# Last layer of a transformer-like chain: int8 rounding without clip and without GpSimd, bias and outlier sums moved, token maxima turned one outlier tile earlier

## The reference, cut to what matters

```python
def _ste_quant_rows(a):
    scale = jnp.maximum(jnp.max(jnp.abs(a), axis=-1, keepdims=True) / 127.0, 1e-08)
    return jnp.clip(jnp.round(a / scale), -127.0, 127.0) * scale

def _linear8bit(x, W, b):
    col_max = jnp.max(jnp.abs(x), axis=tuple(range(x.ndim - 1)))
    outlier = col_max > 3.0
    x_in = jnp.where(outlier, 0.0, x)
    x_out = jnp.where(outlier, x, 0.0)
    return _ste_quant_rows(x_in) @ _ste_quant_rows(W).T + x_out @ W.T + b

h = _linear8bit(x, W1, b1)          # 512 -> 2048
x = x + _linear8bit(h, W2, b2)      # 2048 -> 512
```

## Time and profile before

| | us |
|---|---|
| median of 3 runs | 2096.34 |
| lowest, highest | 2092.91, 2097.01 |
| the profiled execution | 2093.76 |
| its span (first to last instruction) | 2092.0 |

### The profile page before, as it was taken

How to read it: one execution, slowest core, us unless ns; L and a number is a source line. 1 busy time by engine, 2 the same in 40 slices (tenths; PEclk the granted TensorE clock), 3 DMA queues, 4 the chain that set the end, 5 groups by cost and what they waited for, 6 DMA issues and landing times.

```text
span 2092.0 us, 32276 instructions
## 1 busy us (share of the span) xinstructions
PE 1975.2 (94%) x11816; PEld 1673.6 (80%) x11824; DVE 1463.6 (70%) x2973; ACT 1157.9 (55%) x2367; POOL 827.0 (40%) x824
## 2 busy tenths in 40 slices
PE   6999999999889999979999999999998999987986
PEld 4888888888779888867889889889887778765763
DVE  6777787777666666656666666666674577876798
ACT  4766666666235555533655555555561377875543
POOL 6554554452633212053422322311145531544653
PEclk9999999999999999999999999999999999997998
DMA  4101110100211020120110010000001200211200
GB/s 152 51 23 50 51 51 31 51 21 21 89 43 38 21 53 13 29 70 30 41 51 21 21 51 21 26 36 21 24 32 60 68 21 8 75 61 61 101 26 21
DMA packets 35947, 90.76 MB, mean 43 GB/s; under 512 B 17104, under 2 KB 22480, under 8 KB 27856
## 3 DMA queue, kind: packets, MB, share of 16 engines
q1 hardware_dynamic: 35792, 88.70, 12.6%
HBM read 84.49 MB, written 1.05 MB: 41 GB/s over the span
## 4 chain that ended last, share of the span: by engine, by line
PE 81%; DVE 11%; POOL 3%; issue 2%; ACT 2%; DMA 1%; SPq 0%; DVEq 0%; POOLq 0%; ACTq 0%
PE ps_s L317 11%; PE ps_s L319 11%; PE ps_s L318 11%; PE ps_t L945 8%; PE ps_t L317 6%; PE ps_t L319 6%; PE ps_t L318 6%; PE ps_o L317 5%; PE ps_o L319 4%; PE ps_o L318 4%; PE ps_o L1689 3%; PE ps_t L1725 2%; PE ps_s L1675 2%; PE ps_t L952 1%; DVE f_e L1261 1%
## 5 line engine op out<-in xcount | busy, mean ns | idle before, releaser
L998 ACT ACTIVATE l_pt_hi<-ps_t 128x512 fp32r<-128x512 f32 (+1 forms) x512 | 244.4, 515 | 299.9 <-PE ps_t L945 298.7
L1057 DVE TENSOR_REDUCE nmax<-ps_s 128x1 f32<-128x768 f32 x192 | 183.8, 958 | 279.5 <-PE ps_s L319 277.5
L1065 DVE TENSOR_TENSOR l_pt_lo<-ps_t,l_pt_hi 128x512 fp32r<-128x512 f32 (+1 forms) x512 | 281.8, 582 | 4.9 <-ACT l_pt_hi L998 4.9
L1025 ACT ACTIVATE l_p<-ps_s,nmax 128x768 f32<-128x768 f32 x192 | 173.5, 904 | 160.8 <-DVE nmax L1057 160.1
L945 PE MATMUL ps_t<-ident,l_p 128*128 128x128 f32 x1664 | 236.6, 274 | 7.8 <-DVE l_pt_lo L1065 4.0
L317 PE MATMUL ps_o<-l_pt_hi,l_v_hi 128*128 128x256 f32 (+1 forms) x832 | 237.0, 285 | 5.9 <-DVE l_pt_lo L1065 5.9
L355 POOL TENSOR_TENSOR wo_hi<-raw_big,one 128x512 fp32r<-128x512 f32 (+2 forms) x100 | 102.9, 1029 | 346.6 <-PE ps_t L319 333.1
L945 PEld LDWEIGHTS ps_t<-ident,l_p 128*128 128x128 f32 x1664 | 198.3, 140 | 48.3 <-issue 8.3
L319 PE MATMUL ps_o<-l_pt_hi,l_v_lo 128*128 128x256 f32 (+1 forms) x832 | 234.9, 282 | 0.0
L318 PE MATMUL ps_o<-l_pt_lo,l_v_hi 128*128 128x256 f32 (+1 forms) x832 | 234.6, 282 | 0.0
L355 POOL TENSOR_TENSOR wq_hi<-raw_big,one 128x512 fp32r<-128x512 f32 (+1 forms) x104 | 114.0, 1096 | 259.4 <-PE ps_t L319 225.2
(11 more groups left out here) (410 smaller groups left out, 5398.4 us busy)
## 6 DMA issues: line engine op xcount, KB each, us to landing
raw_big<-in_l_wq SPq DMA_DIRECT2D x18, 1024.0 KB, 4.8
raw_big<-in_l_wo SPq DMA_DIRECT2D x18, 1024.0 KB, 4.8
raw_big<-in_f_w SPq DMA_DIRECT2D x7, 1024.0 KB, 4.9
raw_kv<-in_l_wkv SPq DMA_DIRECT2D x12, 512.0 KB, 5.8
raw_f<-in_f_w SPq DMA_DIRECT2D x4, 1024.0 KB, 4.9
q_nat<-in_f_w2n SPq DMA_DIRECT2D x4, 1024.0 KB, 5.1
q_nat<-in_f_w1n SPq DMA_DIRECT2D x4, 1024.0 KB, 4.9
raw_big<-in_l_wq SPq DMA_DIRECT2D x12, 192.0 KB, 3.1
```

Of the source, the lines that this page charges most:

```text
L998: e.activation(sp.pt[u % 2][0][:, k0:k0 + nk, qt * P:(qt + 1) * P], ps_t[p % 2][:, 0:nk * P].rearrange("p (k q) -> p k q", q=P), ACT.Copy) ...
L1025: e.activation(sp.p[:, k % 3, :], sp.p[:, k % 3, :] if l.rope else self.scores_out(k), ACT.Exp, bias=nmax[:, i:i + 1], scale=-1.0 if l.rop ...
L1057: e.tensor_reduce(nmax[:, i:i + 1], self.scores_out(k), AX.X, ALU.max, negate=True).then_inc(s_max, 1)
L1065: e.tensor_tensor(pt[1], ps_t[p % 2][:, 0:nk * P].rearrange("p (k q) -> p k q", q=P), pt[0].bitcast(F32), ALU.subtract).then_inc(s_tlo, 1)
```

## The change

Rounding loses its clip: a product with the reciprocal of the token's maximum over 127 is already at most 127 up to rounding error. `quantise` goes from three DVE instructions to two, and a tile shared with ACT from two DVE instructions (the second waiting for the first) to one. GpSimd's three tiles, their ACT copies and their buffers go. DVE now does tiles 0, 3, 6, 9, 12 and 15 alone, DVE and ACT together the other ten. The bias is added to x before DVE's first hidden tile instead of in the serial stretch; its buffer and its DMA move too. The float part is added to x before the first rounding instead of ahead of tile 11. `turn_largest` stands ahead of the last float tile. At the end GpSimd adds quarters 0 and 2 to x and DVE quarters 1 and 3.

```diff
-        q_b2 = at("q_b2", [P, D], F32, 48)
+        q_b2 = at("q_b2", [P, D], F32, R0 + 88)
-        POOL_TILES = (6, 10, 14)
-        DVE_TILES = (0, 7)
+        DVE_TILES = (0, 3, 6, 9, 12, 15)
+        POOL_OUT = (0, 2)
@@ f3_sp
             load_chunk(2)
+            e.dma_start(q_b2[:, :], A["f3_b2"]).then_inc(s_lay, 16)
...
-            e.wait_ge(s4["rows_int"], 7)
-            e.dma_start(q_b2[:, :], A["f3_b2"]).then_inc(s_lay, 16)
             for t in range(TT):
-                e.wait_ge(s4["finished"], t + 1)
+                if t in POOL_OUT:
+                    e.wait_ge(s4["added"], POOL_OUT.index(t) + 1)
+                else:
+                    e.wait_ge(s4["finished"], t + 1 - sum(p < t for p in POOL_OUT))
@@ f3_pool
-            for i, hb in enumerate(POOL_TILES):
...
+            for i, t in enumerate(POOL_OUT):
+                e.wait_ge(s4["dequantised"], i + 1)
+                e.tensor_tensor(x[:, t, :], x[:, t, :], q_c[:, t, :], ALU.add).then_inc(s4["added"], 1)
@@ f3_pe
+                if j == HT - 1:
+                    e.wait_ge(s4["turned_out"], 8)
+                    e.wait_ge(s4["kept_max"], HT + 1)
+                    turn_largest(out_bank[0])
                 out_second(j)
...
-            e.wait_ge(s4["turned_out"], 8)
-            e.wait_ge(s4["kept_max"], HT + 1)
-            turn_largest(out_bank[0])
@@ parts_of (f3_act)
-                if j in POOL_TILES:
-                    e.wait_ge(s4["rows_int"], 8)
-                    e.activation(q_hk[:, POOL_TILES.index(j), :], h[:, j, :], ACT.Copy, scale=q_mi[:, j:j + 1])\
-                        .then_inc(s4["h_moved"], 1)
@@ quantise (f3_dve)
-                link(e.tensor_scalar(t, t, MAGIC, MAGIC + 127.0, ALU.add, ALU.min))
-                e.tensor_scalar(dst, t, MAGIC - 127.0, -MAGIC, ALU.max, ALU.add).then_inc(done, 1)
+                e.tensor_scalar(dst, t, MAGIC, -MAGIC, ALU.add, ALU.add).then_inc(done, 1)
@@ f3_dve
             e.memset(q_amx[:, :], 0.0).then_inc(s4["kept_max"], 1)
+            e.wait_ge(s_lay, LAY["f3"] + 16)
+            add_row(e, q_b2[:, :], link)
...
             make_diag(diagr, q_tr, True)
-            e.wait_ge(s_lay, LAY["f3"] + 16)
-            add_row(e, q_b2[:, :], link)
+            e.wait_ge(s4["used"], HT)
+            for t in range(TT):
+                last = e.tensor_tensor(x[:, t, :], ring[t], x[:, t, :], ALU.add)
+            last.then_inc(s4["outliers_added"], 1)
...
-                link(e.scalar_tensor_tensor(out=t, in0=h[:, hb, :], scalar=q_mi[:, hb:hb + 1], in1=q_rrow[:, :],
-                                            op0=ALU.mult, op1=ALU.mult))
-                e.tensor_scalar(t, t, 127.0, -127.0, ALU.min, ALU.max).then_inc(s4["h_clipped"], 1)
+                e.scalar_tensor_tensor(out=t, in0=h[:, hb, :], scalar=q_mi[:, hb:hb + 1], in1=q_rrow[:, :],
+                                       op0=ALU.mult, op1=ALU.mult).then_inc(s4["h_scaled"], 1)
+            e.wait_ge(s4["h_int"], n)
+            e.wait_ge(s4["outliers_added"], 1)
             for t in range(TT):
                 e.wait_ge(s4["acc"], t + 1)
-                link(e.scalar_tensor_tensor(out=q_t[:, t % 2, :], in0=acc_i[t], scalar=q_ts[:, t:t + 1], in1=q_s2row[:, :],
-                                            op0=ALU.mult, op1=ALU.mult))
-                e.tensor_tensor(x[:, t, :], x[:, t, :], q_t[:, t % 2, :], ALU.add).then_inc(s4["finished"], 1)
+                last = e.scalar_tensor_tensor(out=q_c[:, t, :], in0=acc_i[t], scalar=q_ts[:, t:t + 1], in1=q_s2row[:, :],
+                                              op0=ALU.mult, op1=ALU.mult)
+                if t in POOL_OUT:
+                    last.then_inc(s4["dequantised"], 1)
+                    continue
+                link(last)
+                e.tensor_tensor(x[:, t, :], x[:, t, :], q_c[:, t, :], ALU.add).then_inc(s4["finished"], 1)
```

More of the change, by code:

```diff
@@ L191, in program @@
         q_c = at("q_c", [P, 4, 512], F32, R0 + 48)
-        q_hk = at("q_hk", [P, 3, 512], F32, 96)
-        q_tp = at("q_tp", [P, 512], F32, 102)
         diagr = at("diagr", [P, 4, P], F32, R0 + 60)
@@ L1883, in program @@
                                          "out_full", "out_kept", "int_full", "int_out", "row_full", "row_out", "largest", "diag",
-                                         "x_int", "summed", "masks", "h_clipped", "h_moved", "h_int", "h_int_dve", "kept_max", "magnitude", "x_magnitude", "hi", "lo", "used", "acc", "finished",
+                                         "x_int", "summed", "masks", "h_scaled", "h_int", "h_int_dve", "kept_max", "magnitude", "x_magnitude", "hi", "lo", "used", "acc", "finished", "added", "dequantised", "outliers_added",
                                          "x_staged")}
-        s_pint = sem("f3_pool_chain")
-        POOL_TILES = (6, 10, 14)
         INT_BEHIND = {9: 0, 10: 1, 12: 2, 13: 3}
         EARLY = len(INT_BEHIND)
-        DVE_TILES = (0, 7)
+        DVE_TILES = (0, 3, 6, 9, 12, 15)
+        POOL_OUT = (0, 2)
         def raw_of(cc):
@@ L2104, in f3_pe @@
             for hb in range(HT):
-                if hb in POOL_TILES:
-                    e.wait_ge(s_pint, 3 * POOL_TILES.index(hb) + 3)
-                elif hb in DVE_TILES:
+                if hb in DVE_TILES:
                     e.wait_ge(s4["h_int_dve"], DVE_TILES.index(hb) + 1)
                 else:
-                    e.wait_ge(s4["h_int"], hb + 1 - sum(p < hb for p in POOL_TILES + DVE_TILES))
+                    e.wait_ge(s4["h_int"], hb + 1 - sum(p < hb for p in DVE_TILES))
                 for t in range(TT):
@@ L2198, in f3_act @@
             for hb in range(HT):
-                if hb in POOL_TILES or hb in DVE_TILES:
+                if hb in DVE_TILES:
                     continue
                 n += 1
-                e.wait_ge(s4["h_clipped"], n)
+                e.wait_ge(s4["h_scaled"], n)
                 t = q_c[:, (n - 1) % 4, :]
@@ L2315, in f3_dve @@
             for hb in range(HT):
[L2316 to L2322, removed]
                 if hb in DVE_TILES:
```

## The result

| | us |
|---|---|
| median of 4 runs | 2079.38 (2077.77 to 2082.74) |
| before, 4 runs | 2095.71 (2092.91 to 2097.01) |
| ratio | 0.9937, 95% interval 0.9925 to 0.9950 |
| profiled execution, its span | 2082.74, 2080.9 |

The change makes the kernel 13.2 us faster by this ratio (10.5 to 15.7); the two medians of four runs differ by more, 16.3 us.

A forecast was written before the change was run, and what follows sets the result against it. The prediction took VectorE feeding TensorE too slowly in the last product as the bound. From a mean of 2095.0 us it took 10.0 for an earlier first scaling, 0 for tail and bias: 2085.0, range 2081.5 to 2089.

The forecast's parts named there:

- TensorE becomes the bound: Last product: TensorE, with 15 tiles from tile 1 on, 12.9 us or more, ends behind VectorE and ScalarE.
- Serial stretch: Between float part and rounding: spread starts 2.1 us earlier, and VectorE's own adds set the rounding's start at 2055.7.
- P: Distance from the first rounding to the first scaling in the last product, forecast at 18.2 us.
- three low tiles: Last product: three tiles at half clock, first scaling 18.2 us behind the first rounding, gain 10.0 us; the value taken.
- two low tiles: Last product: two tiles at half clock, 3.3 us, first scaling 17.4 us behind the first rounding, gain 10.8 us.
- Full clock: Rival: the clock stays full in the last product; gain 12.2 us, time 2082.8, chance 0.22.
- The tail: First scaling to last add: bounds 4.3 to 6.6 us, taken as 5.6, no change.
- the 1.79 row: Earlier profile row for VectorE's adds from SBUF beside GpSimd, 1.79 against 0.69 us alone; would give a tail of 6.6.
- The moved bias: Four adds ahead of hidden tile 0, 2.5 to 7.2 us, costed at nothing because later waits cover them.
- Sum: Whole kernel: -10.0 us up to the first scaling, 0 for tail, 0 for bias; 2095.0 becomes 2085.0.
- 0.93: Chance given to faster by over 0.2%, its cases lying at 2082.8 to 2089 us.
- the case of a longer low clock: Rival: five up to ten tiles of the last product at half clock; time 2086.6 to 2090.7, chance 0.16.

The follow-up runs named there:

- a_clip: Changed kernel with the clip put back in all 16 tiles, GpSimd still silent; ratio 0.9970 to the kernel before.
- a_sum_last: Changed kernel with the sum of the float part moved behind the last rounding; ratio 0.9946 to the kernel before.
- a_warm: Changed kernel with 15 overwritten matmuls between the spread and the first product; ratio 0.9938 to the kernel before.
- s_sums: Kernel before with only the bias add moved ahead of hidden tile 0 and the float sum put in its old place; ratio 0.9987 to before.
- s_noclip: Kernel before with only the clip left out, GpSimd keeping its three tiles; ratio 0.9972 to before.
- s_round: Kernel before with only the rounding changed: no clip, no GpSimd tiles, six tiles on DVE alone; ratio 0.9963 to before.
- a_best: Changed kernel with the float sum behind the last rounding and 8 overwritten matmuls between spread and first product; ratio 0.9935 to the kernel before.

## Why the prediction was right, and where a size was off

- *TensorE becomes the bound.* Right: 10.15 busy of 10.20 us, no wait behind the second tile; a_clip shows the other side.
- *Serial stretch.* Right. VectorE started rounding 2.60 us behind the float part's end, forecast 2055.7 - 2053.15 = 2.55; VectorE's sum set it, not the turn (`q_rrow` was there at 2053.73 + 0.60 = 2054.33, 0.9 us earlier). a_sum_last confirms it from the other side.
- *The rounding and the clock.* P was forecast at 18.2 (three low tiles) and came at 17.89, 17.42 and 17.44. The fall of the clock came as expected, but where it fell differed. In the first trace it came ahead of tile 0, which was low too and cost nothing, because tile 1 waited for ScalarE in any case; tiles 1 and 2 were low and tile 3 in part. In the other two traces it came behind tile 0 and hit tiles 1 and 2, and there P is what the prediction worked out for two low tiles, 17.4. Taking three was a choice, 0.3 to 0.8 us too many. Full clock: forecast 16.0, shown 16.17 by a_warm.
- *The tail* was costed at no change; it is 0.44 shorter, 0.3 net. VectorE's add took 1.20 us, not 1.79: it started 0.61 us behind GpSimd's add and ended 0.55 behind its end. The rule of the Trainium skill (page "SBUF — State Buffer", section "SBUF: two separate sides") that one shuts the other out would give 2075.23 + 0.69 = 2075.92 for the first add; measured 2075.78. For this add the trace agrees with the rule within 0.15 us, and taking the 1.79 row whole would have been wrong. The whole tail of 5.6 that the prediction had from the rule is 0.4 longer than measured. And the rule does not hold here beside every instruction of GpSimd. Before, a multiply with two SBUF inputs that began with GpSimd's multiply ended 0.54 us behind it; one that ran wholly inside GpSimd's two-constant instruction, which reads SBUF too, took no longer than alone:

```profile
2063.26 1.27 POOL L1960 TENSOR_TENSOR q_tp<-q_hk,q_rrow 128x512 f32<-128x512 f32 x1 [0.17 <-POOL hq L1964]
2064.61 2.25 POOL L1962 TENSOR_SCALAR q_tp<-q_tp 128x512 f32<-128x512 f32 x1
```

```profile
2063.28 1.79 DVE L2330 SCALAR_TENSOR_TENSOR q_c<-h,q_mi,q_rrow 128x512 f32<-128x512 f32 x1
2065.74 0.74 DVE L2330 SCALAR_TENSOR_TENSOR q_c<-h,q_mi,q_rrow 128x512 f32<-128x512 f32 x1
```

- *The moved bias* was costed at nothing. Right, at 5.44 us of VectorE in place of 2.5 to 7.2; s_sums shows no wait behind it.
- *Sum.* 10.0 forecast; the traces give 10.6, 11.3, 11.4, of which 0.4 is the tail and most of the rest the low tiles. That the median still left the range I put down to the scatter of the runs, for which I had allowed 2 us either way: with the recorded ratio the forecast's 2095.0 would become 2081.8, inside the range. Spans of the changed kernel in one set of timings ran from 2075.9 to 2080.9 and in another from 2078.6 to 2084.4, and the layer's start alone moved by 4.3 us between two traces. The forecast's level of 2095.0 for before was itself high against the later sets (medians 2091.94, 2091.05, 2090.93 and 2093.04). The prediction also let its 0.93 end at 2089, though the case of a longer low clock, which is part of it, reaches 2090.7.

What stays open: how much of the 2.1 us between s_noclip and s_round comes from the new split of the tiles, why F is 1.4 us longer in s_round, and what sets where the low stretch falls. That no other stretch gained is only as sure as the timings: about 2 us.

## What to carry to other kernels

A chained second instruction on the engine that feeds TensorE can make that engine the bound: here the clip was worth 4 to 6 us. An engine that "helps" beside it can cost more than its share: taking three tiles from GpSimd shortened the product by 1.4 to 2.1 us. So count the feeder's instructions first, then ask who runs beside it. Gains of parts that were measured one by one don't add up once the bound has moved. When TensorE becomes the bound after a short idle stretch, add some tiles at half clock to the sum, and give that term a range: three traces of one program gave a P from 17.42 to 17.89. A sum that must wait for TensorE can stand behind the work that TensorE waits for; the traces of a_sum_last and a_best show this hidden, the timings don't resolve it.

## What the runs showed of the hardware that was not expected

- VectorE's multiply of 128x512 takes 0.70 us in a row with GpSimd silent, and 0.96 beside GpSimd over five. A single one takes up to 1.79 beside GpSimd's multiply and 0.74 inside GpSimd's two-constant instruction. VectorE's own two-constant instruction takes 0.43 alone and took 1.38 beside GpSimd in s_noclip.
- The low stretch differs between traces of one program. After a TensorE wait of 3.27 us the clock was at 0.50 for some 6.6 us, the first of them still in the wait; after a wait of 3.11 us the product began at 1.00 and ran at 0.50 for about 3.3 us from its second tile on. With 15 overwritten matmuls in the wait it stayed at 1.00, and with 8 too, but it also did so once without any, in a_sum_last, after a wait of 2.24 us.
